# Gated expert layer on one core: the shared network's down projection with its weights as the stationary operand, its result turned back over DRAM

## What is computed

```python
# x: (8, 512, 512) f32, one label in 0..4 for each batch element
def _gated_ffn(x, wi0, wi1, wo):
    g = jax.nn.gelu(x @ wi0, approximate=True)        # 512 -> 2048
    l = x @ wi1
    return g * l @ wo                                  # 2048 -> 512
share_out = _gated_ffn(hidden_states, sWi0, sWi1, sWo)
...                                                    # expert_out: the same with Wi0/Wi1/Wo[label]
gate_in = jnp.concatenate([expert_out[:, 0], share_out[:, 0]], axis=-1)
weights = jax.nn.softmax(jax.nn.relu(gate_in @ g0) @ g1, axis=-1)
x + expert_out * w0 + share_out * w1
```

## Time and profile before

| | |
|---|---|
| median of 3 runs | 1966.42 us (1966.16 to 1966.43) |
| the profiled execution | 1965.97 us, its span 1964.2 us |
| PE busy | 1959.2 us, 100% of the span, 11159 matmuls |
| PEld busy | 1728.9 us (88%) |
| DVE busy | 1381.4 us (70%) |
| ACT busy | 958.6 us (49%) |
| POOL busy | 82.5 us (4%) |
| DMA | 178540 packets, 287.12 MB, 146 GB/s mean |

### The profile page before, as it was taken

How to read it: one execution, slowest core, us unless ns; L and a number is a source line. 1 busy time by engine, 2 the same in 40 slices (tenths; PEclk the granted TensorE clock), 3 DMA queues, 4 the chain that set the end, 5 groups by cost and what they waited for, 6 DMA issues and landing times.

```text
span 1964.2 us, 28888 instructions
## 1 busy us (share of the span) xinstructions
PE 1959.2 (100%) x11159; PEld 1728.9 (88%) x11159; DVE 1381.4 (70%) x1670; ACT 958.6 (49%) x1307; POOL 82.5 (4%) x56
## 2 busy tenths in 40 slices
PE   9999999999999999999999999999999999999999
PEld 8988888899998888889999888889999988888998
DVE  8776667789885444578988545458898844545888
ACT  6564444466665332346666533234666653323564
POOL 0000000002010000000101000000010100000000
PEclk9999999999999999999999999999999999999999
DMA  5455445244455344324445534432444453343253
GB/s 161 142 180 204 164 169 203 67 158 142 144 181 197 109 164 152 106 86 140 150 151 167 199 122 145 161 108 76 155 152 146 161 204 130 129 163 105 79 163 113
DMA packets 178540, 287.12 MB, mean 146 GB/s; under 512 B 12002, under 2 KB 93922, under 8 KB 174562
## 3 DMA queue, kind: packets, MB, share of 16 engines
q1 hardware_dynamic: 177858, 284.74, 43.6%
q10 hardware_dynamic: 544, 0.52, 0.1%
HBM read 247.47 MB, written 37.75 MB: 145 GB/s over the span
## 4 chain that ended last, share of the span: by engine, by line
PE 99%; DMA 0%; SPq 0%; DVE 0%; DVEq 0%; issue 0%; ACT 0%
PE ps_outs L503 35%; PE ps_pv L484 18%; PE ps_pv L494 18%; PE ps_c L484 14%; PE ps_c L494 13%; PE ps_c L525 0%; PE ps_outs L525 0%; PE ps_outs L484 0%; DMA a_src<-experts 0%; PE ps_outs L512 0%; SPq L309 0%; DVE s_out L1399 0%; DVEq L154 0%; ACT a_both L861 0%; SPq L356 0%
## 5 line engine op out<-in xcount | busy, mean ns | idle before, releaser
L484 PE MATMUL ps_pv<-xh,a_both 128*128 128x256 f32 x2016 | 383.8, 283 | 0.1
L494 PE MATMUL ps_pv<-xh,a_both 128*128 128x512 f32 x1024 | 336.1, 389 | 0.0
L1015 DVE TENSOR_TENSOR a_both<-a_src,a_both 128x512 fp32r<-128x512 f32 (+3 forms) x221 | 302.0, 1368 | 35.1 <-ACT a_both L739 34.2
L484 PEld LDWEIGHTS ps_pv<-xh,a_both 128*128 128x128 f32 x2016 | 323.7, 192 | 0.4 <-issue 0.3
L484 PE MATMUL ps_c<-xh,a_both 128*128 128x256 f32 x1512 | 293.1, 283 | 0.0
L484 PE MATMUL ps_pv<-xl,a_both 128*128 128x256 f32 x1008 | 285.2, 283 | 0.0
L494 PE MATMUL ps_c<-xh,a_both 128*128 128x512 f32 x768 | 257.9, 389 | 0.0
L739 ACT CAST a_both<-a_src 128x1024 fp32r<-128x1024 f32 (+2 forms) x213 | 250.9, 1184 | 0.5 <-DVE a_src L1039 0.5
L484 PEld LDWEIGHTS ps_c<-xh,a_both 128*128 128x128 f32 x1512 | 244.8, 192 | 2.6
L796 ACT ACTIVATE act<-ps_c 128x256 f32<-128x256 f32 (+1 forms) x191 | 87.0, 455 | 321.9 <-PE ps_c L484 171.4
L494 PEld LDWEIGHTS ps_pv<-xh,a_both 128*128 128x128 f32 x1024 | 192.2, 188 | 40.6 <-ACT ps_pv L886 0.8
(11 more groups left out here) (113 smaller groups left out, 2942.5 us busy)
## 6 DMA issues: line engine op xcount, KB each, us to landing
a_both<-kept SPq DMA_DIRECT2D x168, 512.0 KB, 5.7
a_src<-experts SPq DMA_DIRECT2D x255, 256.0 KB, 3.8
raw_wo<-experts SPq DMA_DIRECT2D x128, 256.0 KB, 2.8
g_sb<-g_rows SPq DMA_DIRECT2D x16, 1024.0 KB, 5.4
raw_wo<-shared SPq DMA_DIRECT2D x64, 256.0 KB, 2.9
kept<-a_both SPq DMA_DIRECT2D x8, 2048.0 KB, 8.4
a_src<-shared SPq DMA_DIRECT2D x32, 256.0 KB, 3.4
kept<-a_both SPq DMA_DIRECT2D x8, 1024.0 KB, 8.7
```

What stands on the lines that cost most here:

```text
L484: mm = nc.tensor.matmul(ps[:, a * HALF:(a + 1) * HALF], a_op[ap][:, i, a, k, :], x_op[xp][:, j, k, h, :], start=(start and a == 0 and k == ...
L494: mm = nc.tensor.matmul(ps, a_op[ap][:, i, a, k, :], x_op[xp][:, i, k, :, :].rearrange("p h t -> p (h t)"), start=(start and k == 0 and q ...
L1015: nc.vector.tensor_tensor(to, of, hi.bitcast(F32), ALU.subtract).then_inc(done, 1)
```

## The change

`turned_down` replaces `down` for the shared network: `wo` is the stationary operand (a column tile of 128) and all 512 tokens of `hidden` are the moving one, so `ps_out[m]` now holds 128 output columns on the partitions and tokens along them. The high and low parts of `hidden` become one tensor `hid`. `load_wo` loads the shared `wo` in another column order: 8 DMAs of 128 x 4 runs of 32 floats (128 B) a step for 2 DMAs of 128 runs of 2 KB.

Since `s_out` is then transposed, `turn_blocks` transposes it in 32x32 blocks on VectorE (8 instructions a batch: 4 of 384 columns, 4 of 128) into free space of `x_src` and `lin`; SP stores the blocks with 8 DMAs (runs of 512 B) into the DRAM scratch `turned`, waits for them, and loads `turned` back into `s_out` (1 MB). This is done in the odd batch's expert pass: at c = 1 for the even batch, at c = 3 for the odd one.

The gate takes the halves in another order: for an even batch the expert half goes first and is done in the shared pass (GATE turn, c = 1); for an odd batch the shared half is first as before. `gate_row` has one row where it had two, so a spread waits for the multiply-reduces before it. `negative` and its four ScalarE instructions go; instead VectorE subtracts `s_out` from the four PSUM tiles (`take_shared`, two at the end of step c = 4 and two at c = 5 of the last batch).

```diff
 def load_wo(n):
     for f in range(2):
-        sp.dma_start(raw_wo[:, f, :], chunk(n, f)[:, WI:CHUNK_W]).then_inc(wo_loaded, 16)
+        to, of = raw_wo[:, f, :], chunk(n, f)[:, WI:CHUNK_W]
+        if is_wide(n):
+            to = to.rearrange("p (q i c) -> p q i c", q=MC, i=MC)
+            of = of.rearrange("p (i q c) -> p q i c", q=MC, i=MC)
+            for q in range(MC):
+                sp.dma_start(to[:, q, :, :], of[:, q, :, :]).then_inc(wo_loaded, 16)
+        else:
+            sp.dma_start(to, of).then_inc(wo_loaded, 16)
...
+def turn_back(b):
+    sp.wait_ge(blocks_turned, (b + 1) * 2 * MC)
+    to = turned[b].rearrange("(j a) d -> a j d", a=32)
+    for of, (j0, j1) in zip(blocks, BLOCKS):
+        for i in range(MC):
+            sp.dma_start(to[:, j0:j1, i * P:(i + 1) * P], of[32 * i:32 * i + 32, :, :]
+                         ).then_inc(turned_stored, 16)
+    sp.wait_ge(turned_stored, (b + 1) * 2 * MC * 16)
+    sp.dma_start(s_out[:, b % 2, :, :], turned[b].rearrange("(m p) d -> p m d", p=P)
+                 ).then_inc(turned_loaded, 16)
...
+        if c == 1 and b % 2 == 1:
+            turn_back(b - 1)
         if c == 1 and b > 0:
             sp.wait_ge(gate_prod_done, (b - 1) * 2 * NC + NC)
-            load_gate(EXPERT)
+            load_gate(1 - first_net(b - 1))
         if c == 2 and b > 0:
             sp.wait_ge(gate_prod_done, b * 2 * NC)
             load_rows(b - 1)
+        if c == 3 and b % 2 == 1:
+            turn_back(b)
...
+def turned_down(m, s, hidden):
+    for f in range(2):
+        for q, (hp, wp) in enumerate(PASSES):
+            mm = nc.tensor.matmul(ps_out[m], wo[s][wp][:, f, m * P:(m + 1) * P], hidden[hp][:, f, :],
...
 def shared_tile(m, h, b, n):
...
-    down(m, n % 2, True, True, hidden_of[h]).then_inc(down_done, 1)
+    turned_down(m, n % 2, hidden_of[h]).then_inc(down_done, 1)
...
+def turn_blocks(b):
+    dve.wait_ge(added, (b // 2 + 1) * PAIR_ADDS)
+    if b % 2 == 1:
+        dve.wait_ge(turned_stored, b * 2 * MC * 16)
+    for to, (j0, j1) in zip(blocks, BLOCKS):
+        for m in range(MC):
+            nc.vector.transpose(to[:, :, 32 * m:32 * m + 32], s_out[:, b % 2, m, 32 * j0:32 * j1]
+                                ).then_inc(blocks_turned, 1)
...
 def between(b, c):
+    if b % 2 == 1 and c == 1:
+        turn_blocks(b - 1)
+    if b % 2 == 1 and c == 3:
+        turn_blocks(b)
     if b > 0:
-        if c == 1:
+        if c == 1 and b % 2 == 0:
             gate_half(b - 1, 0)
...
 def shared_gate(n, c, b):
...
     a_lo(n, 2)
+    if c == 1:
+        gate_half(b, 0)
```

More of the change, by code:

```diff
@@ L121, in reloads, with wo_loads, first_net @@
     return (pair - 1) * STEPS + (q - STEPS + 1)
+def wo_loads(n):
+    pair, q = divmod(n + 1, PAIR_STEPS)
+    return 2 * (n + 1) + 6 * (pair * STEPS + min(max(q - WIDE0, 0), STEPS))
+def first_net(b):
+    return EXPERT if b % 2 == 0 else SHARED
 def a_splits(m, g):
@@ L172, in build @@
         p5 = sb("p5", [P, 2, HALF])
-        hs = [sb(f"hid{p}", [P, 2, 2, TOK], F32R) for p in "hl"]
+        hid = sb("hid", [P, 2, 2, 2, TOK], F32R)
+        hs = [hid[:, :, p, :, :] for p in range(2)]
         s_out = sb("s_out", [P, 2, MC, D])
@@ L280, in build @@
         last_mixed = sem("last_mixed")
-        negative_copied = sem("negative_copied")
+        shared_taken = sem("shared_taken")
+        blocks_turned = sem("blocks_turned")
+        turned_stored = sem("turned_stored")
+        turned_loaded = sem("turned_loaded")
         p4_copied = sem("p4_copied")
@@ L506, in down @@
                 return mm
+            def turned_down(m, s, hidden):
+                for f in range(2):
+                    for q, (hp, wp) in enumerate(PASSES):
+                        mm = nc.tensor.matmul(ps_out[m], wo[s][wp][:, f, m * P:(m + 1) * P], hidden[hp][:, f, :],
+                                              start=(f == 0 and q == 0), stop=(f == 1 and q == 2),
+                                              skip_group_check=True)
+                return mm
             def last_down(m, passes):
@@ L556, in expert_tile @@
                 start = c == 0
[L557 to L561, removed]
+                if b == BATCH - 1 and c == (4 if m < 2 else 5):
+                    pe.wait_ge(shared_taken, m + 1)
+                if c == 0 and b % 2 == 1:
                     pe.wait_ge(added, (b // 2 + 1) * PAIR_ADDS - MC + (m + 1))
@@ L924, in expert_step @@
                     hid_hi(0)
-                if b == BATCH - 1 and c == 1:
-                    for m in range(MC):
-                        negative(m)
                 if very_last:
@@ L1258, in expert_step, with take_shared @@
                         add_tile(m, 1, b - 1, n - 1, t, 0)
+                if b == BATCH - 1 and c in (4, 5):
+                    for m in range(2 * c - 8, 2 * c - 6):
+                        take_shared(m, t)
+            def turn_blocks(b):
[6 more added lines that the diff above has]
+                                            ).then_inc(blocks_turned, 1)
+            def take_shared(m, t):
+                dve.wait_ge(turned_loaded, BATCH * 16)
+                dve.wait_ge(down_done, downs(t) - MC + (m + 1))
+                nc.vector.tensor_tensor(ps_out[m], ps_out[m], s_out[:, 1, m, :], ALU.subtract).then_inc(shared_taken, 1)
             def between(b, c):
+                if b % 2 == 1 and c == 1:
+                    turn_blocks(b - 1)
+                if b % 2 == 1 and c == 3:
+                    turn_blocks(b)
                 if b > 0:
-                    if c == 1:
+                    if c == 1 and b % 2 == 0:
                         gate_half(b - 1, 0)
@@ L1416, in moving_sums, with spread @@
                 difference(P4, P2, P6)
[L1418 to L1426, removed]
+            def spread(b, i):
+                if first_net(b) == (SHARED if i == 0 else EXPERT):
+                    pool.wait_ge(turned_loaded, (b + 1) * 16)
+                    row = s_out[0:1, b % 2, 0, :]
+                else:
+                    pool.wait_ge(out_copied, b * MC + 1)
+                    row = e_out[0:1, 0, :]
+                if b > 0 or i > 0:
+                    pool.wait_ge(gate_prod_done, (b * 2 + i) * NC)
+                nc.gpsimd.partition_broadcast(gate_row[:, :], row).then_inc(row_spread, 1)
             def sum_logits(b):
@@ L1433, in _ @@
                 if b > 0:
-                    spread_shared(b - 1)
-                    spread_expert(b - 1)
+                    spread(b - 1, 0)
+                    spread(b - 1, 1)
                     sum_logits(b - 1)
@@ L1438, in _ @@
                     moving_sums(b + 1)
-            spread_shared(BATCH - 1)
-            spread_expert(BATCH - 1)
+            spread(BATCH - 1, 0)
+            spread(BATCH - 1, 1)
             sum_logits(BATCH - 1)
```

21 lines of the change are left out of this document (11 added, 10 removed).

## The result

| | before | after |
|---|---|---|
| median of 8 runs each | 1965.97 us (1965.53 to 1966.43) | 1972.05 us (1971.13 to 1972.97) |
| span of the profiled execution | 1964.2 us | 1970.2 us |

The ratio is 1.003, 95% interval 1.0019 to 1.0041. The change costs 6.1 us. That is inside the range given, but the forecast was no change, and this is more than the 4 us that counted as none.

What follows compares the result with a forecast made beforehand. PE was taken as the bound, one stream of matmuls without gaps, 1959.2 of 1964.2 us busy. Every term summed to 0 on PE, so span 1964.2 us and a forecast median of 1966.4 us, range 1963 to 1984.

Steps and rivals of the forecast that it cites:

- the term of the 128-byte packets: Shared wo load in a reloaded pass: 20 ns a packet, 5.1 us a step; P1's reload still in time, cost 0.
- The price of an issue: SP's queue at the shared wo load: eight issues at 0.556 us each in place of two in 0.81 us.
- Rival 2: GATE turns after a shared wo load, 21 places: small packets hold up reloads; 77 us, 2044 us; chance 0.09.
- The round trip's sum: Odd expert pass: transposes, stores, load back, gate weights there at T0 + 17.6, just what PE does not see; 0 us.
- rival 1: Odd pass comes late, PE waits: middle 8 us, 1974 us; end 17 + 4 us, 1987 us; chance 0.22.
- The transposes: VectorE at c = 1 of the odd pass: eight cost 2.6 us, replacing 2.8 us of gate_half.
- The edits given at zero: Edits lying under other work, and c = 3's added transposes within PE's spare time: each 0 us.
- Rival 3: Shared down projection: swapped matmuls run closer together, up to 21 us faster, 1946 us; chance 0.04.

Runs made afterwards that it cites:

- the kernel with the two moves in SP's queue: Changed kernel with P4's reload issued ahead of wo and odd batches' gate weights loaded at c = 0, not c = 1: 1966.04 us, 1.0000 of the kernel before.
- the kernel with the gate weights first: Changed kernel with the gate weights' load issued ahead of the turned blocks' store and reload at c = 1 of odd batches: 1975.04 us, 1.0038 of the kernel before.

## Why the prediction was right or wrong

**The step that failed is the term of the 128-byte packets, put at "Cost 0": it cost 4.8 us, at a place that was not looked at.** The prediction went through one `wo` load, in a LIN turn inside a reloaded pass, found 4 us of room for P1's reload, and wrote "Cost 0". Inside the pass that held. At 716.88 the eight issues took 5.18 us (4.4 in the sum), P1's reload was issued at 722.11 and landed 3.9 us later, and PE waited for no reload there. Rival 2 then counted the places at risk as the GATE turns that follow a shared `wo` load, "7 in each of three pairs". The eighth `wo` of a reloaded pass is loaded in the last step of the expert pass ahead of it, and `next_wo` stands there ahead of P4's reload. That eighth place is loss A, 4.8 of 6.1 us, and it was in the trace of before: six reloads, two `wo` DMAs, P4's reload at 615.11, landing with 1.4 us to spare.

**The price of an issue was taken from a row without a backlog.** 0.556 us each is near what the eight DMAs cost where SP's queue is free (4.22 us at 627.42, 0.53 each). Behind six 512-KB reloads they cost 8.51 us, 1.06 each. At 0.556 P4's reload would have been issued at 612.35 + 4.4 = 616.8. Eight DMAs of 512 B ran so with no loss, but with less work for the engines; for 128 B the estimate above leaves 0.3 to 0.9 us. By that estimate the place alone would have cost something, and the price of an issue there made half or more of the 4.8 us.

**Rival 2 had a part of the mechanism, and the wrong turns.** It priced a packet on the DMA engines and decided at 41 ns, for a turn in which they are free at first. Its sign, idle time of PE for a GATE turn's product, did come, in the one GATE turn of each pass that it had not counted. There even packets of 13 ns could use up the 1.4 us that P4's reload had to spare, because the engines were still busy with six reloads. In the stretch from 700 to 760 us the changed kernel shows (DMA share and GB/s at the end):

```profile
700.00:760.00 60.00, 60.00 (x267) 49.67 (x266) 28.49 (x35) 19.02 (x26) 0.00 (x0) 1.00 0.46 134
```

The engines were busy 16 x 0.46 x 60 = 442 us for 8.04 MB. Two steps' `wo`, 8192 packets, are 1.05 MB of it; the other 6.99 MB are 3414 packets of 2 KB at the 95 ns of the prediction, 324 us. That leaves 118 us for 8192 packets, 14 ns each: an estimate that carries the rounding of the shares; the packet records have 13. The prediction took 20, 15 at the least. The Trainium skill ("DMA: Bandwidth & Descriptors", Specifications) has a read-modify-write under 512 B. No price of it shows in these loads: the median packets of 2 KB and 1 KB, 84 and 46 ns, lie on a line that gives 13 ns for 128 B.

**The round trip's sum was right, and its margin of zero was the loss.** Term by term in the second odd pass, with T0 = 878.06:

| step | predicted | measured |
|---|---|---|
| transposes done | T0 + 2.6 | 880.7, T0 + 2.6 |
| eight stores issued | 4.4 us | 880.81 to 886.06, 5.3 us |
| scratch loaded back, issued | T0 + 9.1 | 887.38, T0 + 9.3 |
| row spread, done | T0 + 14.8 | 893.25 + 1.10, T0 + 16.3 |
| gate weights there | T0 + 17.6 | 895.83, T0 + 17.8 |

The issues were longer by 0.9 us. The last store then landed so soon after them that the reload came only 0.2 us late. The row took 1.5 us longer, because the 1 MB from the scratch landed in 5.8 us (4.9 by its like) and the spread took 1.10 us (0.8). The weights were still last. "T0 + 17.6 is just what PE does not see" was true, and the 0.2 us and the differences between passes became 1.0 us over four passes: rival 1 at an eighth of its middle size of 8 us. Its place and its sign were right. That the time lies in the stated range is luck: the range was made wide for rival 1, and 4.8 of the 6.1 us are another loss.

**The transposes.** All of them, from the trace of the changed kernel (least, median and most ns of one, first and last start):

```profile
L1315 DVE STREAM_TRANSPOSE x_src<-s_out x32: 532/535/573, 387.8 to 1891.8; 128x384 f32<-128x384 f32 x32
L1315 DVE STREAM_TRANSPOSE lin<-s_out x32: 266/270/274, 389.7 to 1892.8; 128x128 f32<-128x128 f32 x32
```

From start to start they take 0.47 and 0.19 us (1.88 for four, 0.77 for four), as priced from the ordinary 32-bit operations (0.46 and 0.20). The Trainium skill ("VectorE: DVE Perf Modes", The three transpose paths) gives 311 ns for a 128x128 transpose in bf16; in f32 the 128-column row stays under that with 270, and the wide ones cost 178 ns for each 128 columns. The 5.0 us a batch, the prediction's estimate from that figure, was nearly twice the 2.65 us that a batch took.

**The edits given at zero** (casts, the moved gate half, `negative`, `take_shared`, c = 3) stayed there: the kernel with the two moves in SP's queue keeps all of them and has the time of the kernel before. **Rival 3** fell with the 226.74 ns.

## What to carry to other kernels

When a load is split in more and smaller runs, look at every place where it is issued, the entry and the end of each loop above all, and there at what stands behind it in the issuing queue and how early that landed before. Both prices belong to the state of the queue: that of an issue, to be taken from a row with the same backlog, and the time of the packets on the DMA engines, which is added in full to what stands behind them when the engines are busy. A sum that ends exactly at the spare time is not a zero; here it was 0.24 us a pass, and moving the load that came last one step earlier made it zero.

## What the runs showed of the hardware

- Eight DMAs of 512 packets each kept SP for 8.51 us (7.82 in the kernel before with small runs) behind six 512-KB loads, and for 4.22 us without them. Eight of 128 packets took 4.09 and 3.65 us at the same two places, and two of 128 packets 0.88 us. Backlog and many packets together made the difference. In the first case the slow issues ended just before the last of the six loads landed, and the rest took 0.51 us each.
- A packet's median time on its DMA engine, by the packet records: 84 ns for 2 KB, 46 for 1 KB and 13 for 128 B in the changed kernel, 27 for 512 B in the kernel with eight DMAs of 512 B. That is a straight line down to 128 B.
- After PE had paused for 2.17 us (1112.74 to 1114.91) its matmuls ran at full speed until about 1116.2, then stood 0.427 us apart seven times (0.35 ahead of them, 0.31 behind), at a granted clock of 0.56 from 1117 to 1120, the lower level of 1.2 GHz for most of it, and full speed came back by 1120. The same followed a pause of 2.45 us in the kernel with the gate weights first (clock 0.61 from 627 to 631). Pauses of 1.98, 1.75 and 1.40 us in the changed kernel had no such tail, and neither had 2.06 us. The pauses of 2.17 and 2.45 us so cost about 1.6 us more than themselves; what sets them apart from the one of 2.06 us was not tried.
